# Chunk states of a state-space layer from pair sums in four column groups, and a second chain spread over steps

## What is computed

```python
def ssm(x, A, B, C, D, gamma, beta):            # x: 4 x 2048 x 256, state: 16
    xB = x @ B.T; xD = x @ D.T
    state = 0                                   # per batch, over the 2048 positions
    for t: state = state @ A.T + xB[t]; states[t] = state
    out = states @ C.T + xD
    return layernorm(out) * gamma + beta
def ffn(x, w_gate, w_up, w_down):               # inner width 704
    # fp4(): per block of 16 values, scale = max|.|/6, round to the FP4 grid
    h = silu(fp4(x) @ fp4(w_gate).T) * (fp4(x) @ fp4(w_up).T)
    return fp4(h) @ fp4(w_down).T
x = layernorm(x + ssm(x, ...))
x = layernorm(x + ffn(x, ...))
```

## Time and profile before

| | us |
|---|---|
| median of 3 runs (lowest, highest) | 600.28 (600.22, 601.83) |
| profiled execution, its own time | 601.74 |
| its span, first to last instruction | 599.9 |
| PE busy, share of the span | 572.3, 95% |
| DVE, ACT, POOL busy | 515.0, 472.8, 495.2 |
| mean granted TensorE clock | 0.972 |

### The profile page before, as it was taken

How to read it: one execution, slowest core, us unless ns; L and a number is a source line. 1 busy time by engine, 2 the same in 40 slices (tenths; PEclk the granted TensorE clock), 3 DMA queues, 4 the chain that set the end, 5 groups by cost and what they waited for, 6 DMA issues and landing times.

```text
span 599.9 us, 12742 instructions
## 1 busy us (share of the span) xinstructions
PE 572.3 (95%) x3705; PEld 516.1 (86%) x3705; DVE 515.0 (86%) x1226; ACT 472.8 (79%) x1422; POOL 495.2 (83%) x671
## 2 busy tenths in 40 slices
PE   7999967899999999999999999999999999999974
PEld 6887756799999999999999999999999999999863
DVE  2894126999999999999999999999999999999971
ACT  4454327688998888888888888888888888888753
POOL 1561326999999999999999999999999999998642
PEclk9999966999999999999999999999999999999996
DMA  7733111111122111211111111211111111100001
GB/s 269 266 146 107 33 48 49 47 38 48 50 57 57 57 53 52 57 56 56 56 56 56 56 56 56 56 56 56 56 56 56 55 55 53 53 24 18 19 27 36
DMA packets 46172, 38.33 MB, mean 64 GB/s; under 512 B 6912, under 2 KB 44864, under 8 KB 45120
## 3 DMA queue, kind: packets, MB, share of 16 engines
q1 hardware_dynamic: 46144, 37.99, 20.8%
HBM read 19.50 MB, written 8.39 MB: 46 GB/s over the span
## 4 chain that ended last, share of the span: by engine, by line
PE 87%; DVE 5%; ACT 3%; issue 2%; POOL 1%; DMA 1%; SPq 1%; POOLq 0%; DVEq 0%; ACTq 0%
PE gu L1037 39%; PE turned L1037 18%; PE yb L1037 7%; PE turned L1091 7%; PE gu L967 2%; PE turned L1058 2%; PE yb L937 1%; PE yb L1048 1%; DMA scratch<-in_L_attn_x_dram 1%; PE turned L1102 1%; PE turned L1101 1%; PE turned L967 1%; PE gu L937 1%; DVE scratch L825 1%; PE grid L878 1%
## 5 line engine op out<-in xcount | busy, mean ns | idle before, releaser
L1037 PE MATMUL gu<-wguHi,xtHi 128*128 128x512 f32 (+1 forms) x384 | 151.7, 395 | 2.4 <-DVE xtLo L818 2.3
L1037 PE MATMUL gu<-wguLo,xtHi 128*128 128x512 f32 (+1 forms) x384 | 144.4, 376 | 0.0
L1037 PE MATMUL gu<-wguHi,xtLo 128*128 128x512 f32 (+1 forms) x384 | 144.2, 375 | 0.0
L1037 PE MATMUL turned<-wdHi,htHi 128*128 128x256 f32 x320 | 92.0, 288 | 3.8 <-DVE htLo L854 3.8
L491 POOL TENSOR_TENSOR scratch<-scratch 128x704 f32<-128x704 f32 x64 | 92.3, 1442 | 2.4 <-DVE scratch L839 1.8
L1037 PE MATMUL turned<-wdHi,htLo 128*128 128x256 f32 x320 | 91.7, 287 | 0.0
L1037 PE MATMUL turned<-wdLo,htHi 128*128 128x256 f32 x320 | 90.7, 283 | 0.0
L496 POOL TENSOR_TENSOR scratch<-scratch 128x640 f32<-128x640 f32 x64 | 82.0, 1282 | 9.9 <-DVE scratch L849 9.7
L1037 PEld LDWEIGHTS gu<-wguHi,xtLo 128*128 128x128 f32 x384 | 72.6, 189 | 12.5
L1037 PEld LDWEIGHTS gu<-wguHi,xtHi 128*128 128x128 f32 x384 | 72.6, 189 | 12.3 <-DVE xtLo L818 3.5
L1037 PEld LDWEIGHTS gu<-wguLo,xtHi 128*128 128x128 f32 x384 | 72.8, 190 | 8.5
(11 more groups left out here) (184 smaller groups left out, 1666.0 us busy)
## 6 DMA issues: line engine op xcount, KB each, us to landing
scratch<-in_L_attn_x_dram SPq DMA_DIRECT2D x8, 1024.0 KB, 5.2
xtTile<-xT SPq DMA_DIRECT2D x64, 128.0 KB, 2.3
scratch<-in_L_attn_x_dram SPq DMA_DIRECT2D x64, 128.0 KB, 2.4
out_dram<-scratch SPq DMA_DIRECT2D x64, 128.0 KB, 1.9
stTile<-statesHi SPq DMA_DIRECT2D x128, 8.0 KB, 1.7
stTile<-statesLo SPq DMA_DIRECT2D x64, 8.0 KB, 1.7
scratch<-in_L_ffn_w_down_dram SPq DMA_DIRECT2D x1, 704.0 KB, 6.3
scratch<-in_L_ffn_w_up_dram SPq DMA_DIRECT2D x1, 640.0 KB, 6.2
```

The costliest lines, as they stand in the source:

```text
L1037: ins = nc.tensor.matmul(to, l, r, start=(first and q == 0), stop=(last and q == len(passes) - 1))
```

## The change

- Chunk states in two stages. `pair_sums(b)` forms, for each of the four pairs of neighbouring positions in a chunk, the sum of both with the first multiplied by A once more. A product now has 32 weight columns instead of 128 and writes 32 partitions, pair q into partitions from 32q; 16 products of 256 columns per batch, as before, with q innermost. ACT then copies the bank to SBUF (`sums_copy`), and one product of 512 columns with a 128 by 128 matrix of powers of A (`tMat`, filled by POOL with the identity and by three DMAs) makes the states of two batches. Batches 0, 1, 2 follow rounds 9, 17, 25, batch 3 step 0.
- D and C are the first DMAs, `d_and_c` moves ahead of round 0, the first weight piece is loaded ahead of x's second half; `busy` is made 12 times at the start and for rounds below 14.
- The weight pieces' absolute values stand behind rounds 8, 10, 14, 19, 23 and 27, the groups behind rounds 14, 17, 18, 21, 22, 25 and 28 to 31. DVE's order is written out: pieces, groups and links of p = 0 interleaved.
- The chain p = 1 is spread over tiles 2 to 5, its links within a step behind `layer` on PE and behind `x_grid` on DVE; `last_states(1)` follows ACT's step 2, `states_hi(1)` its step 6, `states_lo(1)` stands in DVE's step 5.

```diff
-    STATES_AFTER = {11: 0, 19: 1}
     POWERS_FROM = 2
-    GROUPS_FROM = max(STATES_AFTER)
-    CHAIN_FROM = GROUPS_FROM + 2
+    PAIR_SUMS_AFTER = {9: 0, 17: 1, 25: 2}
+    SUMS_COPY_AFTER = 18
+    EXPAND_AFTER = SUMS_COPY_AFTER + 1
+    LAST_AFTER = EXPAND_AFTER + 1
+    CHAIN_FROM = LAST_AFTER + 1
     LINKS = ROUNDS + 4
-    ABS_AFTER = {9: (0,), 11: (1, 2), 15: (3,), 19: (4, 5)}
-    PART_FROM = 4 * (HALVES - KH)
-    FILL_STATES = {-1: range(0, 4), 0: range(4, CHUNK)}
-    FILL_CHAIN = {1: tuple(range(LINKS))}
+    ABS_AFTER = {8: 0, 10: 1, 14: 2, 19: 3, 23: 4, 27: 5}
+    GROUP_AFTER = {14: 0, 17: 1, 18: 2, 21: 3, 22: 4, 25: 5, 28: 6, 29: 7, 30: 8, 31: 9}
+    FILL_CHAIN = {2: (0, 1), 3: (2, 3, 4), 4: (5, 6, 7), 5: (8,)}
...
-            load_x(0)
+                sp.dma_start(dRaw[:, :, :], D.rearrange("(k p) d -> p k d", p=P)).then_inc(s_dc, 16)
+                sp.dma_start(cRaw[:, :, :], C.rearrange("(k p) n -> p k n", p=P)).then_inc(s_dc, 16)
+                load_x(0)
...
+            sp.wait_ge(s_tDiag, 1)
+            sp.wait_ge(s_gc, KH)
+            for i in range(2, CHUNK, 2):
+                sp.dma_start(tMat[N * i:N * i + N, 0:N * i],
+                             qRev[:, CHUNK - i:CHUNK, :].rearrange("p a n -> p (a n)")).then_inc(s_tMat, 16)
             load_x(5)
...
+            w_scales(0)
+            w_scales(1)
+            w_round(0)
+            w_scales(2)
+            w_round(1)
+            w_lo(0)
+            w_scales(3)
+            w_round(2)
+            w_lo(1)
+            w_lo(2)
+            w_scales(4)
+            w_round(3)
+            link(0, 0)
+            w_lo(3)
+            link(0, 1)
+            w_lo(4)
+            w_scales(5)
+            link(0, 2)
+            w_round(4)
+            link(0, 3)
+            w_lo(5)
+            link(0, 4)
+            w_round(5)
+            link(0, 5)
+            w_lo(6)
+            link(0, 6)
+            w_lo(7)
+            link(0, 7)
+            w_lo(8)
+            w_lo(9)
             states_lo(0)
...
+            def pair_sums(b):
...
+                for late in range(2):
                     for c in range(KH):
+                        for q in range(CHUNK // 2):
+                            t = CHUNK - 2 - 2 * q + late
+                            ins = nc.tensor.matmul(fBank[b // BPP][2 * N * q:2 * N * (q + 1), cols],
+                                                   gPair[:, c, N * late:N * late + 2 * N],
+                                                   xT[:, t, c, b * CPB:(b + 1) * CPB],
+                                                   start=(late == 0 and c == 0), stop=(late == 1 and c == KH - 1),
+                                                   skip_group_check=True)
+                ins.then_inc(s_sums, 1)
+
+            def chunk_states(p):
+
+                pe.wait_ge(s_sumc, p + 1)
+                pe.wait_ge(s_tMat, 16 * (CHUNK // 2 - 1))
+                nc.tensor.matmul(fBank[p][:, :], tMat[:, :], as_f32(statesHi[:, p * 512:(p + 1) * 512]),
+                                 start=True, stop=True, skip_group_check=True).then_inc(s_local, 1)
...
+            def fill_links(h, m):
+
+                tile = h * CHUNK + m
+                if isinstance(tile, int):
+                    if tile == 1:
+                        chunk_states(1)
+                    for k in FILL_CHAIN.get(tile, ()):
+                        link(1, k)
...
-            chunk_states(BATCH - 1, FILL_STATES[-1])
             gu0, gu1, gu2 = (ffn_up(k) for k in range(3))
-            run(pe, [(h_turn, 6), (gu1, 4), (gu2, 4), (x_turn, 3), (layer, 0), (ffn_down, 6), (gu0, 3)],
-                {step_: [*(lambda ts=ts: chunk_states(BATCH - 1, ts) for ts in (FILL_STATES.get(step_),) if ts),
-                         *(lambda k=k: link(1, k) for k in FILL_CHAIN.get(step_, ()))] for step_ in range(CHUNK)})
+            run(pe, [(h_turn, 6), (gu1, 4), (gu2, 4), (x_turn, 3), (layer, 0), (fill_links, 0), (ffn_down, 6), (gu0, 3)],
+                {0: [lambda: pair_sums(BATCH - 1)]})
```

More of the change, by code:

```diff
@@ L136, in ssm_fp4_ffn @@
         qRev = sb("qRev", [N, CHUNK + 1, N])
-        gPad = sb("gPad", [P, KH, 2 * P - N])
+        gPair = sb("gPair", [P, KH, 3 * N])
+        tMat = sb("tMat", [P, P])
         sRev = sb("sRev", [N, 2 * SUPER, N])
@@ L423, in _ @@
                                     base=0, pattern=[[-1, P]], channel_multiplier=1).then_inc(s_const, 1)
+            pool.wait_ge(s_const, 2)
+            nc.gpsimd.tensor_copy(tMat[:, :], ident[:, :]).then_inc(s_tDiag, 1)
             nc.gpsimd.memset(qPad, 0.0).then_inc(s_qpad0, 1)
@@ L682, in _ @@
                       (x_abs, 3), (ve1, 1), (ve3, 9)],
-                {1: (lambda: last_states(1),), 2: (lambda: states_hi(1),)})
+                {1: (lambda: sums_copy(1),), 2: (lambda: last_states(1),), 6: (lambda: states_hi(1),)})
         @block.vector
@@ L761, in states_lo @@
                                         ALU.subtract).then_inc(s_states, 1)
-            for k in range(len(W_PIECES) + 1):
-                if k < len(W_PIECES):
-                    w_scales(k)
-                if k >= 1:
-                    w_round(k - 1)
-            for u in range(GROUPS_FROM, 4 * HALVES):
-                if u - GROUPS_FROM < len(W_GROUPS):
-                    w_lo(u - GROUPS_FROM)
-                if 0 <= u - CHAIN_FROM < LINKS - 1:
-                    link(0, u - CHAIN_FROM)
+            w_scales(0)
[28 more added lines that the diff above has]
+            w_lo(9)
             states_lo(0)
@@ L863, in add_x1 @@
                                                accum_out=sum3[:, j:j + 1]).then_inc(s_r, 1)
-            run(dve, [(x_grid, 2), (scale_gamma, 0), (x_max, 1), (add_x, 0), (x_scale, 1), (h_lo, 5), (x_recip, 1),
+            def fill_links(h, m):
+                tile = h * CHUNK + m
+                if isinstance(tile, int):
+                    for k in FILL_CHAIN.get(tile, ()):
+                        if k < LINKS - 1:
+                            link(1, k)
+                    if tile == max(FILL_CHAIN):
+                        states_lo(1)
+            run(dve, [(x_grid, 2), (fill_links, 0), (scale_gamma, 0), (x_max, 1), (add_x, 0), (x_scale, 1), (h_lo, 5), (x_recip, 1),
                       (h_sum, 4), (times_up, 3), (h_grid, 4), (x_lo, 2), (h_max, 3), (add_x1, 5), (h_scale, 3),
-                      (x_sum, 1), (h_recip, 3)],
-                {**{step_: [lambda k=k: link(1, k) for k in ks if k < LINKS - 1] for step_, ks in ((0, range(LINKS)),)},
-                 1: [lambda: states_lo(1)]})
+                      (x_sum, 1), (h_recip, 3)])
         @block.tensor
@@ L878, in busy @@
                     nc.tensor.transpose(wbanks[1][:, 0:P], ident[:, :], ident[:, :])
-            busy(16)
+            busy(12)
             def d_and_c():
```

70 lines of the change are left out of this document (36 added, 34 removed).

## The result

The kernel after took 608.55 us (median of 4 runs, 603.67 to 608.62) against 600.49 for the kernel before on the same chip (4 runs, 600.22 to 601.83); the ratio on record is 1.0096, with a 95% interval of 1.0055 to 1.0137 (it is formed from all runs and is not the quotient of the two medians, which would be 1.0134; the same holds for the ratios below, each with its interval in square brackets). So it is slower, by about 1%. The forecast was 601.7 with a range of 594 to 608, so the side that got the larger chance came true, but the median of 608.55 stands 0.5 us beyond the top of the range, and the size was wrong by nearly 7 us. The profiled execution took 608.48 us with a span of 606.7, 6.8 more than the span of 599.9 before.

A forecast was written before the change was run, and what follows sets the result against it. The prediction took PE's work in the first 110 us as the bound; setup +2.1 and filling -0.7 gave +1.4, 603.1 for the profiled execution, which is 1.46 above its median, so 601.7 us, range 594 to 608.

The forecast's parts named there:

- What bounds the kernel now: Whole kernel: PE busy 459.7 of 460 us from 110 to 570 and unchanged there, so the answer lies in the first 110.
- in setup PE has no gap that counts: Setup: PE taken as continuously busy, with two blocks of chunk states of 7.17 and 7.07 us; states ready at 65.0.
- The pair sums: Chunk states on PE: 3.6 us per batch instead of 7.1, with 1.8 and 7.1 as the ends.
- Round 9 stays at 18.8: Start of setup: two DMA issues delay round 0 by 0.9 us, d_and_c leaving round 2 returns 0.7 to 0.9.
- Round 24 at 43.0: Setup on PE: round 24 at 43.0 us instead of 48.97, a gain of 6.0.
- the loads at nothing: Setup: tMat DMAs ahead of x load 5 cost nothing, as long as that load lands in 5 us.
- PE idle for DVE ahead of round 28: Late setup: PE stands still nearly 4 us behind DVE's rounding 5 and link 5; round 28 at 55.9.
- From round 28 to the states: End of setup: rounds of 2.8 us each through engine hops at full clock, from 55.9 to states_lo at 67.1.
- setup falls to the low clock too: Rival, setup: PE's idle time between rounds 27 and 28 lowers the clock, +3.4 us, 605.1; chance 0.17.
- four at once, with slow setup: Rival, setup: all four column groups overlap at 1.8 us a sum while the clock falls, 599.9; chance 0.10.
- the 5.2 us that four groups were to bring in setup: Rival, setup: pair sums 1.8 us shorter three times, of which DVE's order lets 5.2 through; states at 61.9.
- Filling: Filling: second to third layer -9.8 us, links and waits +2.6, +3.6 and +2.9, in sum -0.7.

The follow-up runs named there:

- e8: Kernel before with the pair sums and the product with the powers of A alone, first chain one round and second chain one step later: 604.04 us, 1.0052.
- e2: Kernel after with x loaded first again, d_and_c back at round 2 and 16 busy transposes at the start: 604.14 us, 1.0057.
- e4: Kernel after with idle transposes ahead of the links of rounds 23, 24, 27, 28, 29 and 20 behind the wait for the first states: 604.9 us, 1.0063.
- e11: Kernel after with pair sums ordered so that two column groups take turns, then the other two: 611.42 us, 1.018.
- e12: Kernel after run again without any edit: 607.35 us, 1.0123.
- e3: Kernel after with the 16 products of a pair sum ordered one column group at a time: 616.36 us, 1.0263.
- e5: Kernel after with both repairs, that is e2 with the idle transposes of e4: 602.01 us, 1.0012.
- e6: e5 with 6, 10, 6 and 6 idle transposes behind the layers of tiles 0 to 3 in filling: 600.37 us, 0.9982.
- e9: e6 with its idle transposes re-placed and re-counted to fill every wait of over 0.3 us in its trace: 603.38 us, 1.004.
- e7: Kernel before with only the second chain spread over tiles 2 to 5 and its two conversions moved: 601.8 us, 1.0011.
- e10: Kernel before with idle transposes in filling and around the turns of h of the last two tiles: 602.92 us, 1.0065.

## Why the prediction was off, step by step

**What bounds the kernel now: half right.** The answer did lie in the first 110 us, and the rest kept its time (477.5 against 477.9). But "in setup PE has no gap that counts" was taken to mean that PE bounds it. DVE's 8.8 and 9.8 of 10 in the same stretch stood in the same view, and e8 shows that it takes over at once. A third limit was a load of x: round 16 waits 1.07 us for it in after, and 0.95 to 1.09 in e2, e4, e11 and e12.

**The pair sums: wrong by half.** The taken price was 3.6, measured 1.93, almost the lower end of 1.8. The failing step was the reasoning that the second record of a product "waits for the first, and in the trace no record of PE starts ahead of an earlier one". The traces of e3, e11 and after give 143, 88 and 60 ns a record, so the records of four groups do run beside one another, and records that start in order need not wait for each other. The Trainium skill (TensorE: Matmul & The Clock Gate, Part 3) gives 2.38 times for three column tiles. The runs here agree in kind only: two groups gave 143 / 88 = 1.6 times, four 143 / 60 = 2.4, and three were not run. The estimate of 2.4 us that the prediction formed from it was nearer to 1.93 than the 3.6 that it took. The error was to the good side: some 3.4 us of PE's time ahead of round 24.

**"Round 9 stays at 18.8": wrong, +3.9.** This step failed first and cost most. The sum counted two DMA issues, 0.9 us, where x landed 1.8 later, and it had no term for the clock, 2.1 more. The row that was needed was in the trace of before: its first round took 1.12 us and its second 0.60, so it started at the low rate as well. I read neither as the clock, since the recorded clock says 1.00 in both kernels at that point. With PE idle from 5.7 to 7.5 the low rate stayed until 16.9 in this execution; in others with the same start it ended sooner (e12) or lay later (e3). e2 shows the whole by removal, 4.4 us of the span and 3.2 to 4.4 of the median, against e12 and after.

**Round 24 at 43.0: measured 44.54.** The two errors above nearly cancel: 43.0 + 3.9 - 3.4 = 43.5. The last 1.0 is round 16's wait for x, 1.07 us, where the prediction had put the loads at nothing; its working looked at the load behind the tMat DMAs, and the one ahead of them was late. The third sum at half the clock (3.52) is another 1.6 right behind it. A checkpoint that looks nearly right thus hid three wrong terms.

**PE idle for DVE ahead of round 28: right.** Forecast nearly 4 us with rounding 5 as the cause; measured 0.71 + 3.32 with that addition as the releaser, and with ACT's absolute values ahead of rounding 5, as forecast. Round 28 was forecast at 55.9 and came at 57.64. It is the written order that costs here, and not DVE's load; rounding 5 behind link 5 was not tried.

**From round 28 to the states: 11.2 forecast, 15.0 measured, +3.8.** This is the rival "setup falls to the low clock too" (+3.4, chance 0.17), and it came true: 57 to 71 us ran at 0.53, and e4's removal of it is worth 4.7 with the third sum. In e4, e5 and e6, where the clock stays up here, this way took 11.2 us each time, the very figure of the forecast: the hops were sized rightly, and the clock was the term put at nothing. The forecast had the idle time right and the row of the fall beside it, and still took the full clock for the likeliest. By the same rows the stretch before a fall looked like this one; it deserved the larger chance. Of the case "four at once, with slow setup" (599.9, chance 0.10) the two mechanisms are what happened, and its sum misses 608.55 by the start (3.9), by 3.0 of the 5.2 us that four groups were to bring in setup (they brought 3.4, less the 1.2 below), and by the 1.46 us between before's profiled execution and its median. Part 4 of the same page of the Trainium skill (TensorE: Matmul & The Clock Gate) says that transposes don't count as activity in the same way; here the kernel before, where PE did nothing but transposes up to round 1 and that round took 0.60 us, and e4 and e9, whose transposes kept the clock up, speak against using that rule in this kernel. The fall at 44 us, behind six nearly full us of mostly transposes and small products, is one case in which it could hold, and no run decides it.

**Filling: -0.7 forecast, measured -1.0** to gu0 of tile 2 (116.03 - 72.6 = 43.4 against 109.41 - 65.0 = 44.4), or -0.4 to the layer of tile 7. The mechanism was right too: third layer 4.3 behind the second, waits of 1.58 and 2.19 at the links. e7 shows that it is no gain by itself. The low level from 90 to 101 us was in the sum.

**The sum.** Forecast +1.4, measured +6.8 in the span: +3.9 for the start, -3.4 for the pair sums, +1.2 that round 28 was late beyond these two (1.07 of it is round 16's wait for x), +3.8 for the clock in the last rounds, and -0.1 behind the states (-0.8 against -0.7). 1.4 + 3.9 - 3.4 + 1.2 + 3.8 - 0.1 = 6.8.

## What to carry to other kernels

Before work is taken off the busiest engine, the second busiest is to be read in the same stretch: if it is at 9 tenths, the removal becomes idle time. The loads are to be read with it: a transfer that was early can become the wait. Idle time of TensorE is then not free, since a stretch at half the clock can follow (behind 3.32 us in after and 5.65 in e8 it did, behind 2.62 in e8 it did not), so the forecast must carry a term for the clock behind each gap that the new order makes, the very first one included. And a filler must be shorter than the gap: its price is read from a row with its own shape.

## What the runs showed of the hardware

- A product with 32 weight columns (two records of 256 columns): 143 ns a record with one column group at work (e3), 88 with two (e11), 60 with four (after); 222 with 128 weight columns (before). A narrow product is cheaper even alone.
- A stretch of 3 us or more at the low rate between 7.5 and 24 us in all five executions in which PE pauses for 1.8 to 2.8 us ahead of round 0, at another place in each (until 16.9 in after, until round 3 in e12, rounds 4 to 7 in e3), and in none of the nine without the pause. The recorded granted clock read 1.00 through it in after, and 0.50 for part of it in e12, so durations of like instructions (1.11 or 0.66 for four transposes) are the surer sign.
- Transposes, with nothing else, brought TensorE to the full rate (before: round 1 took 0.60 us) and held it there (e4, e9), at 0.115 us each at the full rate; 16 of them in e9, at 86.58, took 3.62 us at the low one.
- A mean granted clock of 0.993 to 0.997 went with 603 us (e9, e10), and 0.969 with 600 (e6): the clock is a price on work, no aim.
